# A graph layer with kernelised attention: the weight scaling, the edge columns, the key load, the branch and the last feature tile are moved

## The reference

```python
h = relu(layernorm(x))                      # rows, without gain or bias
xn = batchnorm(h, g1, b1)                   # over the 1250 rows
agg = segment_sum(xn[src], dst) / max(deg, 1)
conv = relu(agg @ W_conv + b_conv)
q, k, v = heads(h_dense, Wq / Wk / Wv)      # 256 rows, 8 heads of 64
qf = exp(u - diag - max) / 16 + 1e-6        # u = (t * 64**-0.25) @ proj.T, 256 features
kf = the same with the maximum over rows and features
attn = (qf @ (kf.T @ v)) / (qf @ sum(kf) + 1e-6)
h_attn = (attn @ Wo)[clipped to row 255]    # rows from 256 on all take row 255
out = x + batchnorm(conv + h_attn + h, g2, b2)
```

## Time and profile before

| what | us |
|---|---|
| median of 3 runs | 198.6 |
| the runs | 195.19, 199.04, 198.6 |
| the profiled execution | 196.43 |
| its span in the trace | 194.6 |
| TensorE busy | 168.6 |
| VectorE busy | 133.3 |
| ScalarE busy | 89.2 |

### The profile page before, as it was taken

The page is one execution under the profiler, slowest core; times in us unless marked ns, Lnnn a source line. Parts: engine busy times, 40 slices in busy tenths (PEclk is TensorE's granted clock), DMA queues, the critical chain, the costliest instruction groups (busy, mean ns, idle before and its releaser), DMA issues.

```text
span 194.6 us, 2956 instructions
## 1 busy us (share of the span) xinstructions
PE 168.6 (87%) x1101; PEld 113.4 (58%) x1102; DVE 133.3 (68%) x309; ACT 89.2 (46%) x157; POOL 12.5 (6%) x26
## 2 busy tenths in 40 slices
PE   0488999995999977899999999797999999999631
PEld 0466898743556534455786677584476474654530
DVE  3786799899555838798844508794407897595952
ACT  3257665426876687998422321715614313004030
POOL 5181000072000000000000000000000000000000
PEclk9999999999799999999999999999999999999975
DMA  6999800000061000000000000293000004040124
GB/s 187 383 349 288 281 5 0 0 0 0 5 188 44 0 3 0 0 0 3 2 0 3 0 0 3 104 309 119 0 3 0 0 0 132 5 132 0 49 83 133
DMA packets 11883, 13.69 MB, mean 70 GB/s; under 512 B 1458, under 2 KB 6748, under 8 KB 11868
## 3 DMA queue, kind: packets, MB, share of 16 engines
q1 hardware_dynamic: 11116, 12.44, 20.1%
q10 hardware_dynamic: 432, 0.79, 1.2%
q0 software_dynamic: 320, 0.26, 0.5%
HBM read 10.92 MB, written 2.56 MB: 69 GB/s over the span
## 4 chain that ended last, share of the span: by engine, by line
PE 67%; DVE 13%; ACT 6%; DMA 5%; SPq 4%; issue 3%; DVEq 0%; ACTq 0%
PE bank L927 21%; PE bank L668 14%; PE bank L601 6%; DMA pj<-in_L_gnn_proj 5%; PE bank L709 4%; PE bank L682 4%; PE bank L692 4%; PE bank L622 3%; PE bank L942 2%; PE bank L613 2%; DVE ohb L1037 2%; PE bank L593 2%; SPq L304 2%; PE bank L636 2%; PE bank L645 2%
## 5 line engine op out<-in xcount | busy, mean ns | idle before, releaser
L927 PE MATMUL bank<-r,gh 128*128 128x512 f16 (+1 forms) x120 | 38.1, 339 | 1.3 <-issue 1.3
L668 PE MATMUL bank<-wc,xs 128*128 128x512 f32 (+1 forms) x80 | 38.8, 609 | 0.5 <-DVE kv L1185 0.4
L927 PE MATMUL bank<-r,gl 128*128 128x512 f16 (+1 forms) x120 | 38.2, 338 | 0.0
L389 ACT ACTIVATE r<-bank 128x500 f16<-128x500 f32 x25 | 19.2, 767 | 18.8 <-PE bank L613 17.8
L1037 DVE TENSOR_TENSOR ohb<-iota,bcol 128x1280 f16<-128x1280 f16 x25 | 20.4, 816 | 0.0
L668 PEld LDWEIGHTS bank<-wc,xs 128*128 128x128 f32 (+1 forms) x80 | 13.5, 187 | 11.1 <-issue 10.7
L1175 DVE SCALAR_TENSOR_TENSOR gl<-bank,gh 128x512 f16<-128x512 f32 (+1 forms) x10 | 6.9, 692 | 16.1 <-ACT gh L491 15.8
L927 PEld LDWEIGHTS bank<-r,gh 128*128 128x128 f16 x120 | 11.6, 97 | 10.6 <-issue 1.7
L601 PE MATMUL bank<-hT,r 128*128 128x256 f32 x64 | 17.1, 426 | 0.7 <-issue 0.7
L927 PEld LDWEIGHTS bank<-r,gl 128*128 128x128 f16 x120 | 11.7, 97 | 9.0
L1308 DVE SCALAR_TENSOR_TENSOR r<-bank,cinv,r 128x512 f32<-128x512 f32 (+1 forms) x12 | 7.8, 646 | 12.1 <-ACT r L575 6.8
(11 more groups left out here) (165 smaller groups left out, 268.3 us busy)
## 6 DMA issues: line engine op xcount, KB each, us to landing
xs<-in_x SPq DMA_DIRECT2D x15, 256.0 KB, 5.1
out<-xs SPq DMA_DIRECT2D x8, 256.0 KB
r<-in_L_gnn_Wq SPq DMA_DIRECT2D x1, 1024.0 KB, 7.5
r<-in_L_gnn_Wk SPq DMA_DIRECT2D x1, 1024.0 KB, 11.9
wc<-in_L_gnn_W_conv SPq DMA_DIRECT2D x1, 1024.0 KB, 12.8
wvo<-in_L_gnn_Wv SPq DMA_DIRECT2D x1, 1024.0 KB, 15.1
wvo<-in_L_gnn_Wo SPq DMA_DIRECT2D x1, 1024.0 KB, 5.3
xs<-in_x ACTq DMA_DIRECT2D x3, 256.0 KB, 4.1
```

Source lines behind the costliest of these rows:

```text
L389: act.activation(A16[:, :, p * GW * W:(p + 1) * GW * W].rearrange("p a (q d) -> p q a d", q=GW), bank[p % 2][:, 0:GW * NT * W].rearrange(" ...
L668: last = nc.tensor.matmul(acc[0:n, :], xnT[:, f, i * P:i * P + n], wc[:, f, :], start=(f == 0), stop=(f == FT - 1))
L927: last = nc.tensor.matmul(acc[:, 0:cn], gg[0:n, s, f * P:(f + 1) * P], A16[0:n, s, c0:c0 + cn], start=(s == 0 and gg is gh), stop=(s == NT ...
```

## The change

It makes these edits; the slow path of uncovered edges moves as a whole and is still not entered. VectorE scales W_conv (four instructions) in place of GpSimd. ScalarE copies the two edge columns in place of VectorE, after VectorE has set the flag. SP loads W_k after waiting for the last tile of x, behind the small vectors and `proj`. TensorE's branch stands between the attention's transposes and `heads_out`. In the last feature tile the three chunks are aggregated in a row; the transposes of tile 2 come after them, followed by 14 matmuls whose result is overwritten; ScalarE's queue issues two of the last stores. The orders written out by hand are altered with it, and the list `order` to match.

```diff
+LATE = 14
...
+        order_end += [("agg", FT - 1, c) for c in range(3)] + [("zT", f, j) for f in (FT - 2, FT - 1) for j in range(3)]
...
-            sp.dma_start(wk, w_k.rearrange("(t p) n -> p t n", p=P)).then_inc(wk_in, 16)
             for k, v in enumerate((g1, b1, g2, b2, b_conv)):
...
-            sp.wait_ge(rows_ready, 1)
+            sp.wait_ge(x_in[NT - 1], 16)
+            sp.dma_start(wk, w_k.rearrange("(t p) n -> p t n", p=P)).then_inc(wk_in, 16)
             sp.dma_start(wc[:, :, :], w_conv.rearrange("(t p) n -> p t n", p=P)).then_inc(wc_in, 16)
...
-            pool.wait_ge(crow_ready, 1)
-            for f in range(FT):
-                pool.tensor_tensor(wc[:, f, :], wc[:, f, :], crow[:, :], ALU.mult).then_inc(wc_scaled, 1)
...
+            def edge_columns():                                  # ScalarE, after store_hT(5)
+                acc = landed(act, "cols")
+                act.wait_ge(flag_ready, 1)
+                act.activation(bcol[:, :, :], acc[:, 0:NW].unsqueeze(2).to_broadcast([P, NW, 2]), ACT.Copy)
+                act.activation(vcol[:, :, :], acc[:, NW:2 * NW].unsqueeze(2).to_broadcast([P, NW, 2]), ACT.Copy
+                               ).then_inc(read("cols"), 1)
...
+            c = slice((FT - 1) * P, D)                           # ScalarE, at its end
+            stored(act, "zT", FT - 1, 1)
+            act.dma_start(out[512:1024, c].rearrange("(t p) n -> p t n", p=P), xs[:, 4:8, c]).then_inc(o_out, 16)
+            stored(act, "zT", FT - 1, 2)
+            act.dma_start(out[(NT - 1) * P:N, c], xs[0:LAST, NT - 1, c]).then_inc(o_out, 16)
...
+                    if (f, j) == (FT - 1, 0):                    # TensorE, transpose_z
+                        for k in range(LATE):
+                            nc.tensor.matmul(acc[:, :], cone[:, :], A16[:, 0, 0:512], start=True, stop=True)
...
             def edge_columns():                                  # VectorE
                 acc = landed(dve, "cols")
-                V.tensor_copy(bcol[:, :, :], acc[:, 0:NW].unsqueeze(2).to_broadcast([P, NW, 2]))
-                V.tensor_copy(vcol[:, :, :], acc[:, NW:2 * NW].unsqueeze(2).to_broadcast([P, NW, 2]))
...
+            def scale_weights(f):
+                V.tensor_tensor(wc[:, f, :], wc[:, f, :], crow[:, :], ALU.mult).then_inc(wc_scaled, 1)
...
-            constants()                                          # VectorE's order
-            weight_sizes()
-            edge_values()
-            bn_piece(0)
-            edge_columns()
-            bn_piece(1)
-            one_hots()
-            link(bn_piece(2))
-            bn_mean()
-            diagonals(0)
-            column_scales()
-            bn_scale()
-            one_hots()
+            edge_values()
+            weight_sizes()
+            constants()
+            edge_columns()
+            bn_piece(0)
+            bn_piece(1)
+            link(bn_piece(2))
+            bn_mean()
+            column_scales()
+            bn_scale()
+            one_hots()
+            diagonals(0)
+            for f in range(FT):
+                scale_weights(f)
+            one_hots()
...
+                for f in range(FT - 1):                          # VectorE, last_phase
...
+                y(f, 0)
+                y(f, 1)
+                link(y(f, 2))
+                moments(f)
+                finish(f - 1, 0)
+                scale(f)
...
+                finish(f - 1, 1)
+                finish(f - 1, 2)
                 for j in range(3):
                     finish(f, j)
```

More of the change, by code:

```diff
@@ L497, in _ @@
             act.activation(bw[:, 1, :], mv1[:, :, 1], ACT.Sqrt, bias=epst[:, 0:1]).then_inc(bn_std, 1)
+            act.wait_ge(bn1_ready, 1)
+            normal_xT(0)
             qk(1, 1)
@@ L515, in _ @@
             store()
+            normal_xT(1)
+            high_part(0)
+            landed(act, "k", 1)
+            q_feat(1)
             q_exp(2)
@@ L518, in _ @@
             store()
-            landed(act, "k", 1)
-            q_feat(1)
-            normal_xT(2)
+            high_part(1)
             store()
-            high_part(1)
+            q_feat(3)
+            high_part(2)
             stored(act, "kmax")
+            k_exps(0, 0)
             store()
-            k_exps(0, 0)
             q_exp(4)
@@ L529, in _ @@
             store()
-            q_feat(3)
-            high_part(2)
-            store()
             k_exps(0, 1)
+            high_part(3)
             store()
@@ L537, in _ @@
             store()
-            high_part(3)
+            q_feat(5)
             k_exps(1, 0)
-            store()
-            q_feat(5)
             high_part(4)
             store()
+            normal_xT(2)
             k_exps(1, 1)
@@ L546, in _ @@
             q_feat(7)
+            store()
             high_part(5)
-            store()
             store()
@@ L559, in _ @@
             store()
+            attn_copy(0)
             high_part(9)
-            store()
-            attn_copy(0)
+            while stores[0] < NGRP:
+                store()
             attn_copy(1)
-            store()
             ha_bias(0)
             ha_bias(1)
-            while stores[0] < NGRP:
-                store()
             stored(act, "ha", 1)
@@ L777, in _ @@
             transpose_h(5)
+            project_consts()
+            columns()
             pe.wait_ge(wk_in, 16)
@@ L781, in _ @@
             transpose_h(7)
-            columns()
             transpose_h(8)
             transpose_h(9)
-            diagonal(0, 0)
-            diagonal(0, 1)
+            weight_sums()
             stored(pe, "consts")
@@ L800, in _ @@
             count()
-            inverse_scales()
             values(1, 0)
-            diagonal(1, 0)
-            values(1, 1)
             stored(pe, "k", 1)
             features("uk", kT, 2)
-            project(0, 0)
-            diagonal(1, 1)
-            project(0, 1)
+            values(1, 1)
             features("uk", kT, 3)
             count()
-            features("uq", qT, 1)
-            count()
+            project(0, 0)
+            inverse_scales()
+            project(0, 1)
+            diagonal(1, 0)
             transpose_qf(0)
@@ L816, in _ @@
             project(1, 0)
+            diagonal(1, 1)
+            features("uq", qT, 1)
             count()
+            project(1, 1)
             key_maximum()
-            project(1, 1)
+            count()
+            project(2, 0)
             key_bias()
@@ L860, in _ @@
                 stored(pe, "kv", i)
-            project(7, 1)
             attention(0)
             count()
-            project(8, 0)
-            attention(1)
-            count()
-            project(8, 1)
-            attention(2)
-            count()
-            project(9, 0)
-            attention(3)
+            project(8, 1)
+            count()
+            attention(2)
+            project(9, 0)
+            count()
+            attention(1)
+            attn_T(0)
             count()
             project(9, 1)
-            count()
-            for i in range(4):
-                stored(pe, "attn", i)
-            attn_T(0)
+            attention(3)
+            while counts[0] < NGRP:
+                count()
             attn_T(1)
-            count()
+            uncovered_edges()
             pe.wait_ge(wo_in, 16)
@@ L965, in _ @@
                 aggregate(f, 2)
+            for c in range(3):
+                aggregate(FT - 1, c)
+            transpose_z(FT - 2)
             transpose_z(FT - 1)
@@ L1235, in _ @@
             key_max_spread()
-            q_feat(0)
             one_hots()
```

157 lines of the change are left out of this document (82 added, 75 removed), and 13 rows, old and new, of the table order.

## The result

The changed kernel takes 199.09 us (median of 12 runs, 196.29 to 201.13), the kernel before, run beside it, 198.74 (12 runs, 195.19 to 200.42). The ratio is 1.012 (95% interval 1.006 to 1.018): no gain, rather a loss of 1%. (The executions of a kernel fall into a faster and a slower group; each ratio here compares the faster ones alone, each median takes all.) The profiled execution has a span of 197.1 us where 186.6 was forecast and 194.6 stood before. So 10.5 us have to be accounted for.

A forecast was written before the change was run, and what follows sets the result against it. TensorE was taken as the bound, losing 10.7 us ahead of the aggregates to idling and slow clock; 5.7 there plus 2.3 in the tail, 8.0 off a 194.6 span, gave 186.6, or 190.2 us as median, range 186.5 to 195.0.

The forecast's parts named there:

- Step 5: The branch moved ahead of `heads_out`: waits of 1.9 us against 2.3 and 0.36 covered, 0.8 us gained.
- Rival B: TensorE's clock falls again, behind the wait at 40, at `count` 12 or behind the branch: 1.75 us a fall; 15%.
- signs of being wrong: Late W_conv, clock under 1.00 before the aggregates, counts waiting for stores from 65 to 90, or last stores landing 3 us late.
- Steps 1 to 4: W_conv's scaling, the front, keys behind x and the middle: TensorE 4.4 us ahead, net, at `count` 12.
- early gather: In the front, the last gather landing at 18, some 2 us earlier: 0.5 us allowed, a quarter of that.
- Rival C: In the front, loads come late, W_conv at 28.5 to 31; whole gain gone from 33.3 on, span 196.4; 5%.
- The wait at `count` 12: In the middle, TensorE is there at 86.7, store 10 ends at 87.9: 1.2 us lost.
- Rival A: ScalarE bounds the middle, so the front's gain is lost until store 10: 3 us longer, span 189.6; 20%.
- Step 6: The tail, the last feature tile with its transposes, additions and stores: 2.3 us gained.
- the crowd: In the tail, tile 2's stores, issued only now: 0.25 of the 0.5 us from two queues left to them.

The follow-up runs named there:

- e1: The changed kernel with the load of x for the output held back until the first half of `heads_out` has landed: 196.37 us, ratio 0.994.
- e5: e1 with 20 matmuls, their result overwritten, queued between the last attention transposes and the branch: 195.57 us, ratio 0.996.
- e2: The changed kernel with TensorE's branch back between `heads_out` and the aggregates: 192.1 us, ratio 0.970.
- f2: The changed kernel with the load of x left early and 20 matmuls queued ahead of the branch: 199.54 us, ratio 1.013.
- e8: e2 without the 14 matmuls ahead of the last transposes: 192.45 us.
- f1: e2 with no branch on TensorE, the slow path for overflowing edge lists left out: 192.03 us, ratio 0.973.
- f3: The kernel before with only the scaling of W_conv moved from GpSimd to VectorE: 193.55 us, ratio 0.980.
- e6: e2 with the load of x only behind the first aggregate chunk: 192.98 us, ratio 0.980.
- e7: e2 with the scaling of W_conv on GpSimd again, VectorE's four multiplications gone: 198.09 us.

## Why the prediction was wrong

**Step 5 failed,** by the sentence that the body jumped over is the same, "so it moves and does not vanish", with its 1.29 carried to the new place. That row was no price of a branch; it was what stuck out behind queued work. In every run with the branch the next matmul starts 2.6 to 3.4 us behind the packet of code: after 126.0 to 129.04, e1 124.0 to 127.38, e5 126.0 to 129.21, before 132.0 to 135.0, e2 128.5 to 131.8 (packets to half a microsecond). What differs is how far ahead of TensorE's last matmul the packet moves. Behind `heads_out` it does so 1.7 us (before, 132.0 against 133.71) and 1.8 us (e2) ahead of it, so 1.3 to 1.5 are left to see (0.9 to 1.5 over the runs whose chain has only the branch there). Ahead of the branch at the new place TensorE waits for the last normalisation and then has four transposes, 0.64 us: 4.2 are seen (e1). The load of x adds 3.0 there. (At the old place no run shows that, though it is in flight in the kernel before too; why is open.) The 1.3 became 7.1, that is 5.8 us of the 10.5.

The Trainium skill ("Runtime: NRT & Kernel Launch", instruction fetch) says that a taken branch out of the fetched window stalls the engine; the trace agrees, with a packet of 0.02 MB on the queue for instructions and those 3 us behind it.

**Rival B's mechanism followed at that place.** It had the clock falling behind the branch for 1.75 us each. Behind a gap of 7.1 us it costs 2.9 (10.06 less 7.14), in e1 2.0, in f2 1.7. I took that price from the earlier trace rows, where the loss of 1.75 is 3.5 us at half clock; here the first 5.9 us of `heads_out` (129.0 to 135.0) stand at half clock. These 2.9 are the second term of the miss; a clock under 1.00 ahead of the aggregates was one of the signs of being wrong.

**Steps 1 to 4 held.** No 128x4 operation of VectorE is over 0.3 us, the factors were ready at 38.36 (40.6 forecast, some 2 earlier with an early gather, which came at 19.43), ScalarE waited 2.75 for the flag at 27.83 (2 to 4 forecast), W_conv landed at 23.58 (23 to 25). Rival C is out (its 196.4, besides, was for a landing at 33.3; its own far end, 31, gives 186.6 + 5.7 + 1.75 = 194.1). The wait at `count` 12 is there within 0.13 us. Timeline of after:

```profile
27.83 0.59 ACT L394 ACTIVATE bcol<-bank 128x500 f16<-128x500 f32 x1 [2.75 <-DVE flag L1106]
37.22 0.16 DVE L998 SCALAR_TENSOR_TENSOR bw<-mv,bw 128x4 f32<-128x4 f32 x1
39.49 0.60 PE L621 MATMUL bank<-ohv,ohb 128*128 128x50 f16 x10 [1.28 <-DVE ohv L1054]
88.01 0.41 PE L621 MATMUL bank<-ohv,ohb 128*128 128x50 f16 x10 [1.07 <-ACT r L387]
```

What was off: the last transposes end at 121.91, where the 129.3 less 7.14 and 1.3 leave 120.9, and this is 1.0 us of the miss. Half of it is the allowance for an early gather. The gather came early, but behind a wait of 1.28 at 39.49 the clock fell (0.80 from 38 to 46.6), and `count` 12 runs at 88.01, where 87.9 was forecast without the allowance. In e2, where the gather was waited for and the clock held (a wait of 0.53), it runs at 88.40, so the early gather won 0.4 at most. The other 0.5 I can't place. Rival A was right in kind only: after 88.4 ScalarE holds nothing up.

**Step 6 was right up to the last transfers.** Counted from the aggregates' start (4.1 us later than before), the last additions end at 189.0 where 189.1 was forecast, and the last issue ends 2.3 us sooner than before (194.02 less 4.1, for 192.26). But from start to end it is 58.0 for 59.6: 1.6 gained, not 2.3, the last 0.7 of the miss. The additions and issues of after, then its end by the microsecond (columns as above, the last two DMA share and GB/s):

```profile
190.38 2.72 DVE L1361 TENSOR_TENSOR xs<-bank,xs 128x512 f32<-128x512 f32 x5
190.79 1.31 PE L954 MATMUL bank<-ident,r 128*128 128x128 f32 x10 [0.58 <-ACT r L584]
193.24 0.78 ACTq L590 DMA_DIRECT2D out<-xs  x1
```
```profile
192.00:193.00 1.00, 0.10 (x1) 0.00 (x0) 1.00 (x3) 0.00 (x0) 0.00 (x0) 1.00 0.94 281
193.00:194.00 1.00, 0.00 (x0) 0.00 (x0) 0.10 (x1) 0.00 (x0) 0.00 (x0) 1.00 0.88 236
194.00:195.00 1.00, 0.00 (x0) 0.00 (x0) 0.00 (x0) 0.00 (x0) 0.00 (x0) 1.00 0.98 285
195.00:196.00 1.00, 0.00 (x0) 0.00 (x0) 0.00 (x0) 0.00 (x0) 0.00 (x0) 1.00 0.85 222
```

The stores of tile 2 are late and run together with those of tile 3, and the end is the time to move both: the 0.25 that I left "to the crowd" was 0.7 too little. It is also why e8 loses so little.

The sum: 5.8 + 2.9 + 1.0 + 0.7 = 10.4 of 10.5. With the branch back (e2) the span is 190.0, 3.4 above the forecast, and the median 192.1, within the range: the other edits bring 4.6 us of the 8.0 forecast, and the branch's move cost more than they brought. That e2 lies in the range is in part the range's width. Its 3.4 are 1.4 up to the last transposes (122.31 for 120.9), 0.9 of copy and issue ahead of `heads_out`, 0.2 at the branch and 0.9 behind it.

## What to carry to other kernels

The price of this branch is the fetch of the code behind it, 4.2 us with next to nothing queued (e1), and the wait that a profile shows is only what the queued work leaves visible; so before moving a branch, see what stands between the engine's last wait and the branch at the new place (20 matmuls of 0.2 us hid 3.3 of it, e5) and what the DMA engines carry then. A faster engine starts transfers earlier that it releases: ask of each what it will meet. And a long gap on TensorE can cost a second time in the clock: 2.9 us behind 7.1, 2.0 behind 4.2.

## What the runs showed that I had not expected

- The load of x, on all 16 DMA engines, holds up a packet of code of 0.02 MB, and with it TensorE, by 3.0 us, twice shown (after less e1, f2 less e5), at the new place only: in the kernel before the load was in flight too, and the gap was 1.29.
- The clock near 40 us fell behind waits of 1.28 (after) and 1.23 (f1), not behind 0.53 (e2); yet waits of 1.24 and 1.38 (at 71.86 and 78.00) in the kernel before left it at 1.00, and the like in f3 (1.23 and 1.37, at 68.24 and 74.37) did not; 2.2 us of idle time and transposes left it at 1.00 in e2 and not in e6. The level after such a gap can't be forecast from these runs.
- GpSimd's multiplications stretch VectorE's smallest operations from 0.16 to 1.2 us, the whole length of one of its own; moving 2.5 us of work onto the busier engine gained 6.0 us of span in the new order (e7 less e2).
